# A fused attention, retention and experts kernel: fp32 products of the tail as three float32r products of split operands

## The reference, cut to what matters

```python
x1 = x  + cross_attention(layernorm(x), ctx)     # 16 heads, 4096 keys, mask
x2 = x1 + retention(layernorm(x1))               # 4 heads, dk 64, dv 128
x3 = x2 + experts(layernorm(x2))                 # 8 experts, soft gate, 0.1 threshold

# retention:  q, k, v, g = xn @ Wq.T, xn @ Wk.T, xn @ Wv.T, xn @ Wg.T
#             q, k rotated; o = (q k^T * decay) v; y = groupnorm(o) * silu(g); y @ Wo.T
# experts:    p = softmax(xn @ gate_w + gate_b); w = p where p >= 0.1, normalised
#             sum_e w[e] * (xn @ expert_w[e] + expert_b[e])
```

## Time and profile before

| what | value |
|---|---|
| runs | 218.77, 219.24, 219.28 us |
| span of the profiled execution | 217.6 us |
| TensorE matmul busy | 206.6 us (95%) |
| VectorE busy | 138.9 us (64%) |
| ScalarE busy | 108.2 us (50%) |
| GpSimd busy | 45.0 us (21%) |
| mean granted clock of TensorE | 0.997 |

### The profile page before, as it was taken

The page is one execution under the profiler, slowest core; times in us unless marked ns, Lnnn a source line. Parts: engine busy times, 40 slices in busy tenths (PEclk is TensorE's granted clock), DMA queues, the critical chain, the costliest instruction groups (busy, mean ns, idle before and its releaser), DMA issues.

```text
span 217.6 us, 5773 instructions
## 1 busy us (share of the span) xinstructions
PE 206.6 (95%) x2386; PEld 125.2 (58%) x2386; DVE 138.9 (64%) x283; ACT 108.2 (50%) x231; POOL 45.0 (21%) x56
## 2 busy tenths in 40 slices
PE   8798998899999999989999999999999998999992
PEld 8366654465567666656666543645758854645341
DVE  3483579986582965888985342675643636594783
ACT  2234767587784867878889761424252231101000
POOL 8307776181270500000000010100030103010000
PEclk9999999999999999999999999999999999999998
DMA  6979774355077690650000000000000000000000
GB/s 181 288 201 293 237 211 104 89 140 140 3 185 169 178 364 4 222 171 5 5 5 3 3 0 0 3 2 0 0 0 0 3 2 0 0 24 3 29 27 29
DMA packets 15792, 18.06 MB, mean 83 GB/s; under 512 B 2640, under 2 KB 14864, under 8 KB 15760
## 3 DMA queue, kind: packets, MB, share of 16 engines
q1 hardware_dynamic: 14464, 17.28, 27.2%
q10 hardware_dynamic: 1296, 0.34, 0.8%
HBM read 9.79 MB, written 0.52 MB: 47 GB/s over the span
## 4 chain that ended last, share of the span: by engine, by line
PE 77%; DVE 7%; DMA 4%; SPq 3%; ACT 3%; issue 2%; POOL 1%; DVEq 0%; ACTq 0%
PE bank L819 11%; PE bank L914 11%; PE bank L896 11%; PE bank L1130 10%; PE bank L1002 8%; PE bank L776 4%; PE bank L762 4%; DVE cneg L1730 3%; PE bank L1110 3%; PE bank L964 3%; DMA ctxT<-in_ctxT 3%; PE bank L1071 2%; PE bank L984 2%; DMA qstack<-xbo 2%; ACT prob L1412 1%
## 5 line engine op out<-in xcount | busy, mean ns | idle before, releaser
L1730 DVE TENSOR_REDUCE cneg<-bank 128x1 f32<-128x896 f32 x64 | 67.8, 1088 | 23.9 <-PE bank L819 23.8
L1412 ACT ACTIVATE prob<-bank 128x512 f32<-128x512 f32 x112 | 64.3, 600 | 14.6 <-PE bank L896 13.3
L896 PE MATMUL bank<-qstack,kstack 100*32 100x256 bf16 x896 | 43.8, 273 | 0.9 <-ACT prob L1412 0.5
L819 PE MATMUL bank<-kstack,qstack 97*32 97x448 bf16 x512 | 36.9, 354 | 2.5 <-DVE cneg L1730 0.9
L896 PEld LDWEIGHTS bank<-qstack,kstack 100*32 100x32 bf16 x896 | 23.8, 96 | 19.4 <-ACT prob L1412 3.4
L914 PE MATMUL bank<-prob,vals 128*32 128x256 f32 x448 | 34.8, 381 | 0.0
L574 POOL TENSOR_TENSOR nw<-nw,halves 128x2 f32<-128x2 f32 (+1 forms) x10 | 8.2, 825 | 118.5 <-DVE nw L1613 92.1
L1002 PE MATMUL bank<-w_late,xnT 128*128 128x512 f32 x48 | 23.5, 605 | 0.1
L819 PEld LDWEIGHTS bank<-kstack,qstack 97*32 97x32 bf16 x512 | 12.5, 95 | 9.8 <-DVE cneg L1730 4.4
L1954 DVE SCALAR_TENSOR_TENSOR x_in<-bank,nwts,x_in 128x256 f32<-128x256 f32 x32 | 15.5, 483 | 2.0 <-PE bank L1130 0.7
L914 PEld LDWEIGHTS bank<-prob,vals 128*32 128x32 f32 x448 | 12.8, 109 | 5.8 <-issue 3.8
(11 more groups left out here) (158 smaller groups left out, 250.1 us busy)
## 6 DMA issues: line engine op xcount, KB each, us to landing
kstack<-kpart SPq DMA_DIRECT2D x21, 224.0 KB
w_late<-in_w_ret SPq DMA_DIRECT2D x1, 1536.0 KB
mask_all<-in_mask SPq DMA_DIRECT2D x2, 512.0 KB, 4.4
ctxT<-in_w_exp SPq DMA_DIRECT2D x1, 1024.0 KB
kpart<-in_w_exp SPq DMA_DIRECT2D x1, 1024.0 KB
ctxT<-in_ctxT SPq DMA_DIRECT2D x2, 448.0 KB, 5.2
ctxT<-in_ctxT SPq DMA_DIRECT2D x1, 896.0 KB, 7.0
qstack<-acc SPq DMA_DIRECT2D x12, 64.0 KB, 3.6
```

The source lines that it names most:

```text
L819: mm = pe.matmul(out[j4:j4 + COLS, :], qstack[0:MROW + 1, h, b, qt * P + j4:qt * P + j4 + COLS], kstack[0:MROW + 1, b, h, half_ * HC:(half ...
L896: mm = pe.matmul(out[j4:j4 + COLS, hh * NQ:(hh + 1) * NQ], kstack[0:KROWS, b, h, kt * P + j4:kt * P + j4 + COLS], qstack[0:KROWS, h, b, :] ...
L1412: act.activation(prob[:, n % PROBS, :], bank[:, c.score_bank(u, jj), :], ACT.Exp).then_inc(c["prob_ready"], 1)
L1730: dve.tensor_reduce(cneg[:, st % 2, i:i + 1], bank[:, pair:pair + 2, 0:HC], AXXY, ALU.max, negate=True).then_inc(c["max_read"], 1)
```

## The change

The change replaces each float32 product of the three groups above by three products in the type float32r: high x high, high x low, low x high, where `high` is the operand copied to float32r and `low` the rest.

1. `project_ret`, `logits`, `pair` and `last_two` issue three matmuls for each (t, c) in place of one. The two with the high activations come first in `project_ret`, then a wait for the low ones.
2. ScalarE's `take_xn` (VectorE's `take_stream` for n2, tiles 0 and 1) copies the turned tile to `xn_high` and signals `high_taken`. VectorE's new `take_low` subtracts it from the tile in PSUM, writes `xn_low` and signals `turn_taken`. So `turn_taken` of n2 and n3 tiles comes from VectorE.
3. GpSimd's `split_late` splits `w_ret`, `w_gate` and `w_exp` into high and low parts: four copies and four subtractions, after `stream_and_bias` and a wait for `score_ready` 56, ahead of `late_roots`.
4. `turn_first_half` (step 54) waits for all eight.
5. The high weights lie in the batch 0 half of `kstack`, the low ones over the weights themselves. `v_tok` and `gated` move to `qstack`, `attn`, `tanh_g` and `ropes` to `prob`.
6. `w_ret` and `w_exp` get load semaphores of their own; `late_loaded` counts seven loads, not ten.
7. Some semaphores are merged (`q_rested` and `q_mid`; those of the path that does not run here).

```diff
+            def split_late():
+                pool.wait_ge(s["ret_loaded"], 16)
+                pool.tensor_copy(ret_high[:, :, :], w_ret[:, :, :]).then_inc(s["split"], 1)
+                pool.wait_ge(s["split"], 1)
+                pool.tensor_tensor(ret_low[:, :, :], w_ret[:, :, :], ret_high[:, :, :].bitcast(F32), ALU.subtract).then_inc(s["split"], 1)
...
+                pool.wait_ge(s["experts_loaded"], 32)
+                for c in range(KIN):
+                    pool.tensor_copy(exp_high[:, c, :, :], w_exp[c]).then_inc(s["split"], 1)
+                    pool.wait_ge(s["split"], 5 + 2 * c)
+                    pool.tensor_tensor(exp_low[c][:, :, :], w_exp[c], exp_high[:, c, :, :].bitcast(F32), ALU.subtract).then_inc(s["split"], 1)
...
                 pool.wait_ge(*only.at("max_cut", 4))
                 stream_and_bias()
+                pool.wait_ge(*only.at("score_ready", NU))
+                split_late()
                 late_roots()
...
             def project_ret(t, m, halves=(0, 1)):
-                taken("n2", t)
+                pe.wait_ge(s["high_taken"], t + 1)
                 if t:
                     pe.wait_ge(s[("rope_read", "v_taken", "gated_ready")[m]], t)
+                cols = slice(m * 512, (m + 1) * 512)
                 for c in halves:
-                    mm = pe.matmul(bank[:, 2 + m, :], xnT[:, c, t * P:(t + 1) * P], w_ret[:, c, m * 512:(m + 1) * 512],
-                                   start=(c == 0), stop=(c == KIN - 1))
+                    pe.matmul(bank[:, 2 + m, :], xn_high[:, c, t * P:(t + 1) * P], ret_high[:, c, cols], start=(c == 0), stop=False)
+                    pe.matmul(bank[:, 2 + m, :], xn_high[:, c, t * P:(t + 1) * P], ret_low[:, c, cols], start=False, stop=False)
+                taken("n2", t)
+                for c in halves:
+                    mm = pe.matmul(bank[:, 2 + m, :], xn_low[:, c, t * P:(t + 1) * P], ret_high[:, c, cols], start=False, stop=(c == KIN - 1))
...
             def turn_first_half():
-                pe.wait_ge(s["late_loaded"], 16 * 10)
+                pe.wait_ge(s["late_loaded"], 16 * LATE_LOADS)
+                pe.wait_ge(s["split"], 2 * len(SPLITS))
...
+                def split_product(out, t, c, experts):
+                    high, low = xn_high[:, c, t * P:(t + 1) * P], xn_low[:, c, t * P:(t + 1) * P]
+                    pe.matmul(out, high, exp_high[:, c, experts, :], start=(c == 0), stop=False, skip_group_check=True)
+                    pe.matmul(out, high, exp_low[c][:, experts, :], start=False, stop=False, skip_group_check=True)
+                    return pe.matmul(out, low, exp_high[:, c, experts, :], start=False, stop=(c == KIN - 1), skip_group_check=True)
...
+            def take_low(kind, t):
+                n = t + 1 + (TT if kind == "n3" else 0)
+                dve.wait_ge(s["high_taken"], n)
+                dve.tensor_tensor(xn_low[:, :, t * P:(t + 1) * P], bank[:, turn_bank(kind, t), 0:D].rearrange("p (f q) -> p f q", f=KIN),
+                                  xn_high[:, :, t * P:(t + 1) * P].bitcast(F32), ALU.subtract).then_inc(s["turn_taken"], 1)
...
                     if t == 0:
                         first_stream(1)
                         layernorms("dve_post", x1, range(QT, TT), "n2_ready")
+                    else:
+                        take_low("n2", t + 1)
                     gate_product(t)
...
                 second_stream(0, [lambda: None, lambda: decay_weights(RH + 2), lambda: decay_weights(RH + 3)])
+                take_low("n3", 0)
+                take_low("n3", 1)
                 gate_logits(0)
...
-                add_experts(1, range(0, 4))
+                add_experts(1, range(0, 2))
+                take_low("n3", 2)
+                add_experts(1, range(2, 4))
+                take_low("n3", 3)
                 gate_logits(1)
```

More of the change, by code:

```diff
@@ L9 @@
 I32 = mybir.dt.int32
+F32R = mybir.dt.float32r
 U8 = mybir.dt.uint8
@@ L129 @@
 DVE_CHAIN = 5 * STAGES
+LATE_LOADS = 7
+SPLITS = ["ret", "gate", "exp0", "exp1"]
 PER = {"k_ready": 8, "k_hi": 4, "k_rest": 4, "k_taken": 4, "k_mid": 4, "k_cut": 4, "v_ready": NVP + 2, "v_evac": NVP + 2,
@@ L234, in build, with sb_over @@
     with ExitStack() as ctx:
+        place = {}
         def sb(name, shape, dt=F32):
+            place[name] = nc.sbuf_base
             return ctx.enter_context(nc.sbuf_tensor(name, shape, dt))
+        def sb_over(of, first, name, shape):
+            return nc.alloc_sbuf_tensor_at(name, shape, F32R, offset=place[of] + first)
         def sem(name):
@@ L352, in build @@
                  kpart_room[:, 0:2 * NE * D].bitcast(F32).rearrange("p (e n) -> p e n", e=NE)]
-        late0 = kstack[:, 0, :, :].rearrange("p h k -> p (h k)").bitcast(F32)
+        ret_cols = KIN * (2 * D + 2 * NV)
+        ret_high = sb_over("kstack", 0, "ret_high", [P, KIN, 2 * D + 2 * NV])
+        ret_low = sb_over("w_late", 0, "ret_low", [P, KIN, 2 * D + 2 * NV])
+        exp_high = sb_over("kstack", 4 * ret_cols, "exp_high", [P, KIN, NE, D])
+        exp_low = [sb_over(of, 0, f"exp_low_{of}", [P, NE, D]) for of in ("ctxT", "kpart")]
+        gate_high = sb("gate_high", [P, KIN, NE], F32R)
+        gate_low = sb("gate_low", [P, KIN, NE], F32R)
+        xn_high = sb_over("wq", 0, "xn_high", [P, KIN, TT * P])
+        xn_low = sb_over("k_full", 0, "xn_low", [P, KIN, TT * P])
+        late0 = qstack[:, :, :, :].rearrange("p h b q -> p (h b q)").bitcast(F32)
+        late3 = prob[:, :, :].rearrange("p n q -> p (n q)")
         late1 = kstack[:, 1, :, :].rearrange("p h k -> p (h k)").bitcast(F32)
@@ L625, in queries_cut @@
                 pool.wait_ge(s["q_hi"], n)
[L626 to L629, removed]
+                pool.tensor_tensor(full, full, part[:, 0, :], ALU.subtract).then_inc(s["q_rest_mid"], 1)
+                pool.wait_ge(s["q_rest_mid"], 2 * n - 1)
+                pool.tensor_copy(part[:, 1, :], full).then_inc(s["q_rest_mid"], 1)
+                pool.wait_ge(s["q_rest_mid"], 2 * n)
                 pool.tensor_tensor(part[:, 2, :], full, part[:, 1, :], ALU.subtract).then_inc(s["q_cut"], 1)
@@ L1129, in pair @@
                     for c in halves:
-                        mm = pe.matmul(bank[:, PAIR_BANKS[m % 4], :], xnT[:, c, t * P:(t + 1) * P],
-                                       w_exp[c][:, 2 * pr:2 * pr + 2, :], start=(c == 0), stop=(c == KIN - 1),
-                                       skip_group_check=True)
+                        mm = split_product(bank[:, PAIR_BANKS[m % 4], :], t, c, slice(2 * pr, 2 * pr + 2))
                     if KIN - 1 in halves:
@@ L1141, in last_two @@
                         for c in range(KIN):
-                            mm = pe.matmul(bank[:, PAIR_BANKS[m % 4], 0:D], xnT[:, c, (TT - 1) * P:TT * P], w_exp[c][:, NE - 2 + i, :],
-                                           start=(c == 0), stop=(c == KIN - 1))
+                            mm = split_product(bank[:, PAIR_BANKS[m % 4], 0:D], TT - 1, c, slice(NE - 2 + i, NE - 1 + i))
                         mm.then_inc(s["pair_ready"], 1)
@@ L1443, in take_xn @@
             def take_xn(kind, t):
-                take_turn(kind, t, xnT[:, :, t * P:(t + 1) * P], bank[:, turn_bank(kind, t), 0:D].rearrange("p (f q) -> p f q", f=KIN))
+                assert TURNS[len(takes)] == (kind, t)
+                act.wait_ge(s["turned"], len(takes) + 1)
+                act.copy(xn_high[:, :, t * P:(t + 1) * P], bank[:, turn_bank(kind, t), 0:D].rearrange("p (f q) -> p f q", f=KIN)
+                         ).then_inc(s["high_taken"], 1)
+                takes.append((kind, t))
             def take_at(t):
                 act.wait_ge(s["turned"], TURN_AT["at", t] + 1)
-                act.activation(xnT[:, 0, t * P:(t + 1) * P], bank[:, turn_bank("at", t), 0:P], ACT.Identity, bias=bv[:, 0:1]).then_inc(s["at_half"], 1)
+                act.activation(xnT[:, 0, t * P:(t + 1) * P], bank[:, turn_bank("at", t), 0:P], ACT.Identity, bias=bv[:, 0:1])
                 take_turn("at", t, xnT[:, 1, t * P:(t + 1) * P], bank[:, turn_bank("at", t), P:2 * P], bias=bv[:, 1:2])
```

61 lines of the change are left out of this document (35 added, 26 removed).

## The result

The changed kernel takes 222.08 us (median; 221.21, 221.97, 222.19, and 226.38, a disturbed run that the ratio leaves out) against 219.26 us for the kernel before. The ratio is 1.0111, 95% interval 1.0080 to 1.0143. The forecast was 213.8 us with a range of 210.8 to 217.2: wrong sign, and outside the range. The profiled execution took 221.97 us with a span of 220.1, against 217.6 before, at a mean granted clock of 0.992.

A forecast was written before the change was run, and what follows sets the result against it. TensorE was taken as the bound, its matmuls filling 95% of the span. Gains of 3.7 and 2.2 us less 0.5 for waits gave 5.4: span 217.6 to 212.2, plus 1.6 makes 213.8 us, range 210.8 to 217.2.

The forecast's parts named there:

- the neighbourhood: VectorE's instructions in the loop beside GpSimd's splits: predicted to cost nothing, from maxima of 1084 ns against a mean of 1088.
- GpSimd's splits: In the loop from about 88.6 us: 22.9 us of work ending at 111.5, 13.6 us of cover, cost nothing.
- Rival 2: GpSimd late: copies and subtractions at half rate, splits end at 134.4, time 223.8; chance 0.04.
- TensorE's records: Float32r products in the tail: one clock a column, three in 0.645 us, each full old product saving 0.215 us.
- rival 1: Float32r records in the tail take two clocks a column, each old product costs 0.42 us more, about 242; chance 0.09.
- Stages (a) to (c): From 128 us through `project_ret(3, 2)`: gains of 1.05, 1.9 and 0.85 us, sum 3.8.
- The wait ahead of `project_ret(2, 0)`: TensorE stalls 0.7 us there for `rope_read` of tile 1, at 143.88; a sign of the prediction.
- Stage (d): n3, tiles 0 and 1, up to 189.0 us: summed gain 3.7 us by its end.
- The chain of the gate: Logits, gate's weights, group norm to the turn at 182.67: tile 0's savings become idle time, chain 0.3 us later.
- (e): After 189.0 us: 1.3 us gained up to `biases(2)`, then 0.9 with VectorE the bound; 2.2 in all.
- The tail in all: The whole tail: 3.7 and 2.2 us gained, 0.5 off for some seven new waits, 5.4 us.
- Rival 5: More idle time in the tail lowers TensorE's granted clock; 5 us at 1.2 GHz costs 2.5, 216.3; chance 0.04.

The follow-up runs named there:

- the two-operand form: The changed kernel with the cast of each cut written as a maximum of the tensor with itself, two SBUF operands; 223.08 us, ratio 1.0167.
- the copies: The gated kernel with two more GpSimd copies of 1536 elements of `w_ret` placed where the cut of the maxima comes; 218.42 us, one run.
- the gated kernel: The changed kernel with GpSimd's subtractions cut in pieces that wait for VectorE's sixth and seventh cut of the maxima, same results; 216.84 us, ratio 0.9880.
- the experiment on records: The gated kernel with eight float32r matmuls of 512 columns and eight bf16 ones of 256 behind TensorE's last one; 214.92 us, one run.
- gated and filled one: The gated kernel with six float32r matmuls that nothing reads, where TensorE waits for batch 1's group norm; 215.79 us, ratio 0.9855.

## Why the prediction was wrong

**The step that failed.** "VectorE's maxima from PSUM take 1084 ns beside a GpSimd cut, against a mean of 1088 over all 64, so I give the neighbourhood nothing", and of the cut, by the line of the Trainium skill that it cites (GPSIMD Engine Reference, Specifications): "those VectorE has in the loop are of 8 elements, so by that rule too it is nothing here". The first half holds for what it saw: the maxima still take 1.09 us each beside the subtractions. The second half took the size of VectorE's instruction as the measure, which was the prediction's own step: the line that it cites gives no size, and it names VectorE's 2-port modes beside the two SBUF inputs. It is no measure: a small instruction that comes in the middle of a GpSimd one is held until that one ends, so the price is the rest of GpSimd's. That is up to 6.74 us, on one of the most urgent instructions of the loop, since the next tile's scores wait for it. In the five holds of which rows show both ends (two casts in the changed kernel, the two-operand form, the third instruction beside the copies, the gated kernel's 0.27) VectorE's instruction ends 0.02 or 0.03 us behind GpSimd's; in six more in the traces it is 0.02 to 0.04.

The Trainium skill states the rule (SBUF — State Buffer, Who interferes with whom): some VectorE forms and GpSimd's instructions share one port pair under an exclusive lock, the first to issue has it for its whole instruction, and the other "fully blocks". The same section excepts VectorE's reductions. This case's trace agrees in both: 3.34 us for the cast, 1.09 for each reduction that runs beside a subtraction. By that rule the price of a cut in the middle of the first subtraction would have been up to its whole length, 6.5 us by the earlier trace rows.

**What the view of before could not show.** In the loop before, GpSimd did nothing from 75 to 125 us, and so no row had a cut beside it. The neighbourhood was bounded from one side only, by a reduction from PSUM. "Idle engine" was taken for free cover. One hint was there: where GpSimd did work in the loop before, it had been released by the cut's last instruction ([7.97 <-DVE mpart L1758] in the earlier trace rows, 13.7 us of such waits in the earlier trace rows), by waits for `max_cut` in its program, so its work began right behind a cut. The changed kernel puts its splits behind a wait for the scores, and that order is gone. Whether it had been meant for this purpose no row says. The missing end of the bound was in the rows all the same: 6.5 us of subtraction across an instruction in a chain that TensorE waits for. With the 5.5 us that was measured in the loop, the prediction's own tail would have given 212.2 + 5.5 + 1.6 = 219.3, no change; the rest up to 222.1 is mostly the tail's shortfall, with the 0.6 us behind the last addition.

**Step by step.**
- GpSimd's splits: 111.5 predicted, 111.4 measured; a copy 0.90 ns an element (1.04 predicted), a subtraction 2.19 (2.11). Rival 2 is out.
- TensorE's records: about half of a float32 record's 0.43 us, as predicted, so rival 1 is out. But the spacing is 0.230 us and not 0.213, for 256 columns 0.118, for 8 columns 0.11. A block of two products mostly takes 1.46 to 1.52 us from start to start of what follows. About 0.1 of that is a longer first spacing, which blocks of before have too (208.18 to 209.14 is 0.96, where 0.86 is the rule), so the saving of a block is some 0.35 us and not 0.43.
- Stages (a) to (c): 3.8 us predicted, 2.59 measured up to the root at 173.58. The 24 products of the projections save 0.045 less each, 1.1 us of the missing 1.2. The size of this term is measured in the experiment on records; that it explains the shortfall is worked out, not shown. The wait ahead of `project_ret(2, 0)` is 0.70 us, as forecast, but the trace puts it down to ScalarE's copy of the high half, not to the rotation.
- Stage (d): 3.7 predicted by 189.0, 1.98 measured up to the root at 194.51.
- The chain of the gate: "the chain is 0.3 later", measured 0.62. Leaving the low half out gives 0.51 of it back. TensorE idles 1.30 us ahead of group norm's turn; 1.5 predicted.
- The end: VectorE does become the bound. It has one sum and eight additions twice, 9.2 us, without a gap:

```profile
206.93 0.42 DVE L2028 TENSOR_TENSOR x_in<-mask_all,bank 128x256 f32<-128x256 f32 x1 [0.72 <-PE bank L1208]
207.39 4.12 DVE L2022 SCALAR_TENSOR_TENSOR x_in<-bank,nwts,x_in 128x256 f32<-128x256 f32 x8
211.55 0.42 DVE L2028 TENSOR_TENSOR x_in<-mask_all,bank 128x256 f32<-128x256 f32 x1
212.00 4.12 DVE L2022 SCALAR_TENSOR_TENSOR x_in<-bank,nwts,x_in 128x256 f32<-128x256 f32 x8
```

  Ahead of it VectorE idles 0.72 us, where it idled 1.23. 2.2 us were predicted for (e), 1.58 measured from the last root on: 0.91 from this sum on, as predicted, and 0.67 before it in place of 1.3.
- The tail in all: 5.4 us predicted, 3.56 measured. The 0.6 behind the last addition comes off that in this profile, but two kernels with the same end differ by 0.7 there.
- Rival 5 named the granted clock in the tail, by idle places there. In the changed kernel the clock did fall, but in the loop, behind a wait that I had priced at nothing, and it cost 1.4 to 1.6 us. The fall in the tail that the rival describes came in two of the other kernels, behind an idle place of 1.3 us, and cost 1.7 us (12.87 for 11.19).

Nearly without the holds on the cut the forecast would have been 3.0 us off and right in sign: the gated kernel takes 216.84 and lies inside the range. Of the versions with the full result and more than one run the gated and filled one has the lowest median, 215.79 us, 1.5% under the kernel before; that it is faster than the gated one is not shown.

## What to carry to other kernels

Before idle time of GpSimd is used, list what VectorE issues beside it and who waits for each of these, however small; the price of a hold is what is left of GpSimd's instruction, not the size of VectorE's. A fall of TensorE's clock behind the wait can come on top (1.4 to 1.6 us here). If such an instruction is urgent, cut GpSimd's work into pieces and start each long piece right behind VectorE's urgent one, by a semaphore. A neighbour's cost is bounded only by a row of the same kind of instruction, with its operands in the same memory.

## What the runs showed of the hardware

- A hold ends with GpSimd's instruction: 8 elements took 3.34, 1.81, 3.33, 0.94 and 1.44 us where 0.16 is usual. GpSimd's copies held VectorE as its subtractions did. Reductions from PSUM were not held (1.09 us), nor was a copy out of PSUM (0.30 us at 91.67, inside a subtraction of 6.74). A fill of GpSimd's, which only writes (1.80 us at 17.47 in the kernel before), did not hold a VectorE instruction with its operands in SBUF (0.16 us at 17.90).
- After 2.67 us of idle time in 5, in three pieces of 0.5 to 1.3 us, TensorE's granted clock fell from 1.00 to a mean of 0.66 over the next 5 us. In the gated kernel it fell to 0.56 behind a single idle place of 1.28 us; of the six kernels with that place it fell in two and not in four. Behind the copy beside the cut (1.75 us idle in 5) it stayed at 1.00. No rule follows from these rows.
- Float32r streams 0.45 ns a column at 512 columns and 0.46 at 256, where bf16 has 0.43.
